# Splitting the next layer's projection weights one layer ahead, one group per body, in a six-layer attention stack

## What is computed

```python
def attn_layer(x, Wqkv, qs, ksc, Wo):
    q, k, v = jnp.split(x @ Wqkv, 3, -1)          # 16 heads of 64
    q = l2norm(q) * qs; k = l2norm(k) * ksc
    q = q * cos * scale + rotate_half(q) * sin * scale
    k = k * cos * inv + rotate_half(k) * sin * inv
    out = local_attention(q, k, v)                # window 32, softmax
    return out @ Wo
def ffn_layer(x, g, bln, W1, b1, W2, b2):
    xn = (x - mu) / jnp.sqrt(var + 1e-05) * g + bln
    a, gate = jnp.split(xn @ W1 + b1, 2, -1)      # 341 columns each
    return a * gelu(gate) @ W2 + b2
for i in range(6):
    x = attn_layer(shift_tokens(x), Wqkv[i], ...) + x
    x = ffn_layer(shift_tokens(x), ..., W1[i], ...) + x
```

## Time and profile before

| what | value |
|---|---|
| median of 3 runs | 4092.55 us (4092.03 to 4094.78) |
| time of the profiled execution | 4086.93 us |
| its span, first to last instruction | 4085.1 us |
| mean granted clock of TensorE over the span | 0.981 of full speed |
| busy share PE, DVE, ACT, POOL | 93%, 86%, 80%, 75% |

### The profile page before, as it was taken

One profiled execution on the slowest core, in us unless ns is written; L12 is line 12 of the kernel. 1 busy time (PEld: TensorE's weight loads), 2 busy tenths in 40 slices (PEclk: granted clock), 3 DMA queues, 4 the chain that ended last, 5 costly groups with the idle time before them and its releaser, 6 DMA issues. The chain is left out here.

```text
span 4085.1 us, 101499 instructions
## 1 busy us (share of the span) xinstructions
PE 3804.2 (93%) x30384; PEld 3094.1 (76%) x30384; DVE 3499.8 (86%) x11903; ACT 3250.3 (80%) x11174; POOL 3061.3 (75%) x3387
## 2 busy tenths in 40 slices
PE   7888887799999999999999999999999999999997
PEld 5777776578777778777778877878777777777875
DVE  5677776699999999999999999999999999999995
ACT  1555555589898889888989888989888988888985
POOL 2333333588888888888888888888888888888883
PEclk9999999799999999999999999999999999999998
DMA  4222222000000000000000000000000000000000
GB/s 152 79 83 83 83 83 72 22 5 2 2 2 2 28 2 2 2 2 26 4 2 2 2 7 23 2 2 2 2 28 2 2 2 2 7 3 2 2 2 22
DMA packets 76219, 86.71 MB, mean 21 GB/s; under 512 B 13622, under 2 KB 69396, under 8 KB 74836
## 3 DMA queue, kind: packets, MB, share of 16 engines
q1 hardware_dynamic: 75732, 80.87, 6.1%
HBM read 45.33 MB, written 35.52 MB: 20 GB/s over the span
## 5 line engine op out<-in xcount | busy, mean ns | idle before, releaser
L1272 ACT ACTIVATE p<-p,mx 128x128 f32<-128x128 f32 x3072 | 1192.8, 401 | 3.5 <-DVE mx L1357 2.8
L1450 POOL TENSOR_TENSOR rot<-rot,rn 128x512 f32<-128x512 f32 x768 | 805.0, 1048 | 293.3 <-ACT rn L1287 292.4
L1461 POOL TENSOR_TENSOR rot<-own_crossed 128x512 f32<-128x512 f32 x768 | 989.1, 1288 | 0.1
L1446 POOL TENSOR_TENSOR p<-p,ri 128x512 f32<-128x512 f32 x768 | 802.9, 1046 | 24.1 <-DVE ri L1396 24.1
L1357 DVE CUSTOM_DVE_ANT_0 p<-bank_pair,band_f 128x128 f32<-128x128 f32 x3072 | 704.7, 285 | 30.4 <-issue 22.2
L1272 ACT ACTIVATION_READ_ACCUMULATOR p<-p,mx 128x1 f32 x3072 | 612.7, 199 | 0.0
L454 PE MATMUL bank<-wqkv_hi,xs_lo 128*128 128x512 f32 x1152 | 556.6, 483 | 50.9 <-DVE own_crossed L1390 47.6
L1305 ACT ACTIVATE sq<-bank 128x512 f32<-128x512 f32 x768 | 452.6, 589 | 160.0 <-PE bank L456 159.3
L1371 DVE TENSOR_REDUCE ss<-sq 128x8 f32<-128x512 f32 x768 | 521.9, 680 | 9.1 <-ACT sq L1305 9.1
L1408 DVE COPY pTl<-bank 128x512 f32<-128x512 f32 x768 | 511.7, 666 | 16.9 <-PE bank L1176 8.0
L1385 DVE TENSOR_TENSOR own_crossed<-bank,rot_tab 128x512 f32<-128x512 f32 x768 | 522.4, 680 | 0.2
(11 more groups left out here) (198 smaller groups left out, 7353.4 us busy)
## 6 DMA issues: line engine op xcount, KB each, us to landing
pos_scratch<-pos_sb SPq DMA_DIRECT2D x32, 1020.0 KB, 4.4
sc<-pos_scratch SPq DMA_DIRECT2D x32, 512.0 KB, 4.0
wqkv_raw<-in_L_ffn_Wqkv SPq DMA_DIRECT2D x6, 1536.0 KB, 6.8
ctx_sb<-in_ctx SPq DMA_DIRECT2D x32, 128.0 KB, 3.5
wo<-in_L_ffn_Wo SPq DMA_DIRECT2D x6, 512.0 KB, 4.0
mrow<-in_mask_BxS_fk SPq DMA_DIRECT2D x1, 2048.0 KB, 7.7
x_all<-in_x SPq DMA_DIRECT2D x4, 512.0 KB, 8.7
out<-res SPq DMA_DIRECT2D x8, 256.0 KB, 2.3
```

What stands on the lines that cost most here:

```text
L1272: last = nc.scalar.activation(p[:, j, h, :], p[:, j, h, :], ACT.Exp, bias=mx[:, j, h:h + 1], scale=-1.0, accum_out=psums[:, j, h:h + 1])
L1446: nc.gpsimd.tensor_tensor(p[:, j, :, :], p[:, j, :, :], ri[:, j, :].unsqueeze(2).to_broadcast([128, G, T]), ALU.mult).then_inc(L["pn"], 1)
L1450: nc.gpsimd.tensor_tensor(rot[:, (k - 8) % 4, :, :], rot[:, (k - 8) % 4, :, :], rn[:, (k - 8) // 2 % 4, (k - 8) % 2, :].unsqueeze(2).to_br ...
L1461: nc.gpsimd.tensor_tensor(rot[:, (k - 7) % 4, :, :], own[:, (k - 7) % 4, :, :], crossed[:, (k - 7) % 4, :, :], ALU.add).then_inc(L["rot0"], 1)
```

## The change

The query and key weights get two sets of `hi` and `lo` tiles, chosen by the layer's parity; the value weights keep one set. The raw tile shrinks from the whole of Wqkv to two slots of one group each, and the single 1536 KB load becomes six loads of 256 KB, each waiting until the group two before it has been split. Groups 0 to 3 of layer l+1 are now split during layer l, in bodies 2 to 5, one group per body: ACT rounds at k = 12, POOL subtracts at k = 14. Groups 4 and 5 stay in body 0, where they were. W1 is rounded by ACT (body 1, k = 13), and POOL subtracts it in two halves of 341 columns, at k = 15 of body 1 and at k = 0 of body 2. To make room, the values' ring shrinks from 16 to 12 units, and the output's staging tiles share memory with `own_crossed`. SP's loop over the layers is written out.

```diff
+        wqk = (sb("wqk_hi", [128, 2, 2, INNER], F32R), sb("wqk_lo", [128, 2, 2, INNER], F32R))
+        wv = (sb("wv_hi", [128, INNER], F32R), sb("wv_lo", [128, INNER], F32R))
-        wqkv_raw = sb("wqkv_raw", [128, 3, INNER])
+        wqkv_raw = sb("wqkv_raw", [128, 2, 2 * G * DL])
...
+        def load_weight_group(sp, l, e):
+            w = Wqkv[bass.ds(l, 1)].rearrange("a p n -> (a p) n")
...
+            if l + e > 1:
+                wait_apart(sp, L["wqkv_split"], l * WEIGHT_GROUPS + e - 1)
+            sp.dma_start(dst, src).then_inc(L_raw[e % 2], 16)
...
-        v_sb = sb("v_sb", [128, 16, G, DL])
+        VALUES = 12
+        v_sb = sb("v_sb", [128, VALUES, G, DL])
...
+            def ahead(self, k):
+                if self.k != k or self.l == LAYERS - 1 or not 2 <= self.q < 2 + UB:
+                    return None
+                return self.q - 2
...
             def next_layer(l):
-                wait_apart(sp, L["wqkv_split"], l * WEIGHT_GROUPS)
-                load_wqkv(l)
...
                 load_w2(l)
+                if l + 1 < LAYERS:
+                    wait_apart(sp, L["proj_qk"], l * UNITS)
+                    for e in range(WEIGHT_GROUPS):
+                        load_weight_group(sp, l + 1, e)
...
-                if at.renew() and k < UB:
-                    if k == 0:
-                        act.wait_ge(L["wqkv_in"], 16 * (l + 1))
-                    round_group(k)
+                e = at.ahead(12)
+                if e is not None:
+                    round_group(l + 1, e)
+                if at.layer_start(1) and k == 13:
+                    act.wait_ge(Fm["w1_in"], 16 * (l + 1))
+                    if l > 0:
+                        act.wait_ge(Fm["a"], 3 * QUADS * l)
+                    nc.scalar.activation(w1_hi[:, :], w1_raw[:, :], ACT.Copy).then_inc(Fm["w1_hi"], 1)
...
-                if at.renew() and 0 < k <= UB:
-                    keep_rest(k - 1)
+                e = at.ahead(14)
+                if e is not None:
+                    keep_rest(l + 1, e)
                 if at.renew() and k in (6, 8):
-                    keep_rest(UB + (k - 6) // 2)
-                if at.layer_start(1) and k == 14:
...
-                    nc.gpsimd.tensor_copy(w1_hi[:, :], w1_raw[:, :]).then_inc(Fm["w1_hi"], 1)
-                if at.layer_start(1) and k == 15:
-                    pool.wait_ge(Fm["w1_hi"], l + 1)
-                    nc.gpsimd.tensor_tensor(w1_lo[:, :], w1_raw[:, :], w1_hi[:, :].bitcast(F32), ALU.subtract).then_inc(Fm["w1_split"], 1)
+                    keep_rest(l, UB + (k - 6) // 2)
+                if at.layer_start(1) and k == 15 or at.layer_start(2) and k == 0:
+                    wait_apart(pool, Fm["w1_hi"], l + 1)
+                    cols = slice(0, FF) if k == 15 else slice(FF, 2 * FF)
+                    last = nc.gpsimd.tensor_tensor(w1_lo[:, cols], w1_raw[:, cols], w1_hi[:, cols].bitcast(F32), ALU.subtract)
+                    if k == 0:
+                        last.then_inc(Fm["w1_split"], 1)
```

More of the change, by code:

```diff
@@ L433, in emit @@
                         wait_apart(sp, S1["ctxT_mm"], u0 - 1)
+                    if isinstance(first, int) and 0 < u0 < WEIGHT_GROUPS // 2:
+                        for e in (2 * u0, 2 * u0 + 1):
+                            load_weight_group(sp, 0, e)
                     sp.dma_start(ctx_sb[:, k % 2, :], ctx_in[bass.ds(u0, 1)].rearrange("a t c -> t (a c)")).then_inc(S1["ctx_in"], 16)
@@ L1040, in first_attention @@
             def first_attention():
-                load_wqkv(0)
+                for e in range(2):
+                    load_weight_group(sp, 0, e)
                 load_scales(0)
@@ L1131, in emit @@
                             c = 2 * w + h // 2
-                            last = nc.tensor.matmul(oT_ps[rows, c * T:(c + 1) * T], v_sb[:, u % 16, h, :], pTl[:, u % 4, h, :], start=True, stop=True)
+                            last = nc.tensor.matmul(oT_ps[rows, c * T:(c + 1) * T], v_sb[:, u % VALUES, h, :], pTl[:, u % 4, h, :], start=True, stop=True)
                     last.then_inc(L["PV"], 1)
@@ L1294, in emit @@
                     act.wait_ge(L["proj"], at.pair(9) + 1)
-                    if at.again(9, 16):
-                        act.wait_ge(L["PV"], at.pair(9) - 7)
-                    nc.scalar.activation(v_sb[:, (k - 9) % 16:(k - 9) % 16 + 2, :, :].rearrange("p u h n -> p (u h n)"), v_ps[:, :], ACT.Copy).then_inc(L["v"], 1)
+                    if at.again(9, VALUES):
+                        act.wait_ge(L["PV"], at.pair(9) - VALUES // 2 + 1)
+                    nc.scalar.activation(v_sb[:, n(9) % VALUES:n(9) % VALUES + 2, :, :].rearrange("p u h n -> p (u h n)"), v_ps[:, :], ACT.Copy).then_inc(L["v"], 1)
                 if at.renew() and k in (5, 7):
-                    round_group(UB + (k - 5) // 2)
+                    round_group(l, UB + (k - 5) // 2)
                 if on(4):
@@ L1518, in _ @@
             first_ffn()
-            with sp.Fori(1, LAYERS) as l:
+            for l in range(1, LAYERS):
                 next_layer(l)
```

54 lines of the change are left out of this document (30 added, 24 removed).

## The result

The changed kernel takes **4027.6 us** (4027.5 to 4028.6, 4 runs), the kernel before 4092.3 in the same session: ratio 0.9845, 95% interval 0.9828 to 0.9862, **1.55% faster**. I had said 4066, 4048 to 4084: the direction was right, the gain was more than twice the forecast. Five layer starts give 64.7 us in the medians, 58.3 between the two profiled executions (4086.9 and 4028.6).

A forecast was written before the change was run, and what follows sets the result against it. PE, almost never idle in mid-layer, was taken as the bound, with 12.3 us lost per layer start. Terms 0.75 + 4.7 + 0.2 - 0.5 = 5.15 per layer, 26 us for five: 4092.55 to 4066, range 4048 to 4084.

The forecast's parts named there:

- That the stall is DVE against POOL, and worth most of the start: At each layer start DVE's `rot_x` stands still while POOL works; PE loses 7.9 of the start's 12.3 us there.
- POOL is ahead at k = 5 and 6: Layer start: earlier POOL goes idle, DVE's tables get in then, PE's wait falls from 7.9 to 3.2 us: gain 4.7.
- the hole at 6.23 us: Layer start: POOL idle from 6.23 to about 6.9 us behind `sq`, before `xn_lo`, some 0.6 to 0.8 us.
- rival C: Layer start: both tables slip in between POOL instructions, PE's wait 0.8 us, no slow clock: 4050 us, chance 0.13.
- Half clock, gain 0.2: Behind PE's wait at a layer start: half clock loses 1.0 us, of which 0.8 stays; gain 0.2, bounds 0 and 1.0.
- W1, loss 0.5: Bodies 1 and 2: the subtraction's second half delays DVE's bias copies, PE waits 0.82 us longer in three of five layers.
- Groups 0 to 3, gain 0.75: Body before a layer start: moving four roundings and subtractions out of k = 0 to 4 removes its 0.75 us excess.
- Pairs and loads 0: Twenty bodies' added ACT rounding and POOL subtraction fit idle time, and loads are issued early enough: cost 0.
- rival D: Added roundings and subtractions are not hidden: twenty bodies at 1.9 us cost 38 us, 4104 us, chance 0.07.
- B: Layer start: `xn_lo` is issued first, `rot_x` waits to about 9.9 us, PE gains only 1.2: 4085 us, chance 0.13.
- A: The main forecast for the whole kernel holds: 4066 us, own range 4058 to 4073, chance 0.60.

## Why the prediction was wrong

- **That the stall is DVE against POOL, and worth most of the start:** right. Without the tables the kernel before takes 38 us less; with POOL's four subtractions cut it takes 44 us less.
- **"POOL is ahead at k = 5 and 6", gain 4.7: the step that failed.** My sum let DVE in only where POOL is idle, the hole at 6.23 us, because `rot_x` had failed at every end before. In the changed kernel it needed no hole: `rot_tab` and `rot_x` took the next ends, at about 3.0 and 4.0 us behind `sq`. PE starts at 6.04, not 8.47; the term measures 7.9 - 0.8 = 7.1. This is rival C, to which I gave 0.13: it had 3.0, 4.0 and 6.1. I took eight missed ends for a property of `rot_x` and of the lock; they come with a POOL that is late and has run long without idling, which the change removes. Four extra POOL instructions bring them back (4070.9 us), and cutting four removes them (4041.7 us). The hole that I forecast was there (POOL idled for 0.28 us ahead of `xn_lo`), but nothing waited for it any more.
- **Half clock, gain 0.2:** mis-sized. PE's remaining wait of 0.6 leaves the clock at 1.00, where it was 0.50 behind the wait of 7.95. Body 0 takes 0.95 more than a quiet body, of which 0.8 is the later start. On the mean of five it fell by 8.4 (76.2 to 67.8), and 7.1 of that is PE's earlier start. The other 1.3 is what I had put at 0.2 of 1.0; the clock accounts for it, as 3 us at 0.50 cost some 1.5 us (an estimate from the row above).
- **W1, loss 0.5:** the second step that failed; the sign was wrong. I kept the copies' hits and misses as they were and added the half. Body 1 fell from a mean of 69.6 to 67.35: a gain of 2.3. The new order changes what POOL runs when the copy is issued, and all five copies got in early. I had the bound (a gain of 1.3 if all are let in early) but left out the clock that comes with it.
- **Groups 0 to 3, gain 0.75:** right, the body before a start went from 67.66 to 66.84, a gain of 0.8. **Pairs and loads 0:** right, 66.85 in a body with a pair. Neither rival D (4104) nor B (4085) came about. One slip in the chances changes nothing: A, C and half of B add up to 0.80, and the 0.84 for "faster" needs over half of D, which I had described as slower.

Per layer: 0.8 + 7.1 + 1.3 + 2.3 = 11.5, five times 57.5, and 58.3 were measured between the profiled executions. Of the 6.3 per layer that my sum of 5.15 missed, 2.4 lie in the step on the tables, 1.1 in the clock that hangs on it, and 2.8 in the W1 term: two misjudged entries of DVE, not one. C's 4050 was also too high, since it kept the W1 loss (2.8 per layer, 14 us) and since I added the 5.6 us by which the runs before lay above their profiled execution; the changed kernel's median lies 1.0 below its own.

**What stays open:** how it comes that DVE is passed over in the full kernel. Shown there: more POOL instructions ahead of this place bring the stall, fewer remove it. Not told apart: POOL's lateness and the length of its unbroken run. Neither decides alone, since in the same long run `rot_tab` gets in ahead of `ssc` and `rot_x` stands. The size of the product does not decide, nor the place of issue within POOL's instruction by itself (0.12 us into it the table stood with three additions, 0.15 into it it entered in the changed kernel, and 0.55 into it it stood in the kernel before). In 318 trials with the engines alone, satisfied waits, broadcasts, a short instruction, busy neighbours and up to 12.6 us of a burst did not bring it. A longer run, and DVE's work on PSUM ahead of the tables, were not tried there.

## What to carry to other kernels

A stalled two-input VectorE instruction can cost far more than the GpSimd instruction it meets, and how much goes with how late GpSimd is and how long it has worked without idling. When a wait repeats in every layer, compare it with the places where the same instruction met the same engine and got in, and ask what differs there before forecasting that it fails again. Taking GpSimd work out of the stretch ahead of such an instruction (four subtractions per layer cut short here) was worth 44 us; reordering around it was worth 0 to 4.

## What the runs showed of the hardware

- A waiting VectorE product (two inputs in SBUF) was passed over at 7 GpSimd ends (8.6 us) when GpSimd was 0.27 us later, and 14.7 instead of 5.9 us into an unbroken run, than where it entered at the next.
- Issued up to 7.8 us into such a run, 50 products of 50 entered at the next end; issued at 14.7 us or more, 32 of 65 entered before GpSimd idled, 30 of them just ahead of a 128x16 `TENSOR_SCALAR` and none ahead of a 128x512 instruction.
- An entry at a GpSimd end finished about 0.15 us (128x128), 0.55 (128x512) or 0.03 (copy) behind it, in the full kernel and alone, and behind the 128x512 product the GpSimd instruction that had begun took 1.49 instead of 1.04 us. The Trainium skill, SBUF — State Buffer, "Who interferes with whom", says that whichever of the two is issued first holds the shared pair for its whole instruction while the other blocks. Read as a wait for one instruction, that agrees with the 318 trials and the changed kernel (1.29 and 1.52 us), but not with `rot_x` in the kernel before (9.24 us).
